# Query and key projections of a decoder layer branch round their low-half pass, with a common mantissa taken out of the scales

## Chip, cores and metric

One core of one Trainium2 chip runs the whole program. The metric is the device time of one execution in microseconds (us), from runs of the same program on the same inputs. TensorE (PE), VectorE (DVE), ScalarE (ACT), GpSimd (POOL) and SyncE (SP, which here only issues DMAs) each run their own list of instructions in order and wait for each other by semaphores.

## What is computed

A decoder layer with three parts, each followed by a residual sum and a layer norm: self-attention of 16 heads with a head dimension of 128 and 4-bit weights, a cross-attention with top-k, and a gated feed-forward part. Two sequences (b = 0, 1) of 512 tokens, model width 512. The change concerns the self-attention:

```python
def _mxfp4_matmul(x, codes, scales, block_size=BLOCK):
    w = codes * jnp.repeat(scales, block_size, axis=0)
    return x @ w
...
q = _mxfp4_matmul(x, wq_codes, wq_scales) + bq
k = _mxfp4_matmul(x, wk_codes, wk_scales) + bk
v = _mxfp4_matmul(x, wv_codes, wv_scales) + bv
...
scores = jnp.einsum('bqhd,bkhd->bhqk', q, k) / jnp.sqrt(jnp.float32(HEAD_DIM))
attn = jax.nn.softmax(scores, axis=-1)
```

A code is one of 0, 0.5, 1, 1.5, 2, 3, 4, 6 with a sign; a scale belongs to 32 rows of a column. In the inputs the scales of wv and wo are powers of two. Those of wq are powers of two times 2.869, those of wk powers of two times 2.863 (`factors` in the inputs' code), so each of these two tensors has one mantissa in all its 16 x 2048 scales.

## The kernel before

Every fp32 operand of a matmul is split in two halves of a reduced format: `hi`, a rounded copy, and `lo`, what the rounding left. A product is then three passes, lo by hi, hi by hi and hi by lo (`three`), and a 512-deep contraction of a 128 x 512 tile is 12 matmuls. Where the weight's `lo` is zero, one pass is nothing. For wv and wo the kernel tests this as it runs: `check_lo` notes the `lo` tile of each prepared piece, `run_checks` lets ACT sum its absolute values into a column of `mag`, `run_sums` adds the columns over partitions with a small matmul and puts the sum into `flag` by way of ACT, and `mm_if` loads the flag to a register of PE and branches round the matmuls with the weight's `lo` if it is zero. Before the change wq and wk pieces are not tested, and `proj_qk` always issues all 12.

A weight piece goes through `piece_a`: SP loads codes (`RAW`) and scales (`SCL`), POOL multiplies them, ACT writes `hi`, and POOL (DVE at the start and for wv) writes `lo`. The `lo` instruction is held back in `pend` until the next piece or until `flush`. Four `RAW`/`SCL` buffers rotate.

The attention is one loop over i = 4j + qt: j counts 32 pairs of head and sequence (`HB`), qt the four tiles of 128 queries. I call the four steps of one j a round. In this order the loop issues, for each step: the normalisation of the next tile (`recip`, `norm`, DVE), in the first two steps a projection for round j+1 (`proj_qk(j + 1, 0)` for q, then `(j + 1, 1)` for k), in the first step attention by values of round j-1 (`av`, 12 matmuls, which waits for the last transposed tile of that round), in the last two steps the output projection (`proj_o`, 4 matmuls with the branch taken round 2) and in 14 of the rounds a value projection (`proj_v`, 8 matmuls and 4 branched round), the transposes of tile i, the scores of tile i+2 (3 matmuls), then the evacuations by ACT (`hi`) and DVE (`lo`), the exponential of tile i+2 on ACT (`softexp`), and at the end the pieces to prepare. In the trace the instructions of a projection read R, those of `proj_v` read WV,R, those of `proj_o` WO,OT, those of `av` PT,V and those of the scores QK. DVE's row maximum of the scores is L405, its `norm` L422, its `lo` of the transposed tile L441, of a projection L340; ACT's exponential is L412. A projection's result goes to one of three PSUM banks in rotation (`fbank`).

Ahead of the loop stands a start written out by hand: load and prepare head 0, `proj_first`, two tiles of scores, the pieces of wv, then `prep_qk(1, 0)` and `prep_qk(1, 1)`, the four `proj_v(0, 0, tt)`.

Of the kernel before, what the change touches and what calls it, by code (L numbers as in the profile page):

```python
# [62 lines left out]
def decoder_layer(nc, xT, xn, wq, sq, wk, sk, wv, sv, wo, so, bqk, bv, bo,  # L63
                  xwq, xwo, ctxT, ctxn, scal, wg, wu, wd, out):
    with ExitStack() as top:
# [164 lines left out]
        def run_sums():  # L230
            while sums and sums[0][0] < now[0]:
                _, key = sums.pop(0)
                first, n, col, ts = FL[key]
                k, ps = fbank()
                o = ps[0:1, 0:n]
                t = pe.add(lambda e, o=o, first=first, n=n: e.matmul(o, ones[:, 0:1], mag[:, first:first + n],
                                                                  start=True, stop=True),
                           flat([ts, t_one, bank[5 + k]]), True)
                t = op(act, lambda e, o=o, col=col, n=n: e.activation(fsum[:, col, 0:n], o, ACT.Copy,
                                                                       accum_out=flag[:, col:col + 1]), t)  # L240
                bank[5 + k] = t
                T[("flag", *key)] = t

        def flag_of(key):
            c = FL[key][2]
            return flag[0:1, c:c + 1].bitcast(I32), T[("flag", *key)]

        def piece_a(key, hi, lo, src, ssrc, sview, free, em, el):
# [4 lines left out]
            ts = scl_s[k].load(SCL[:, k, 0:sview], ssrc, raw_free[k])  # L253
# [9 lines left out]
            def b():  # L263
# [3 lines left out]
                if key[0] != "qk":  # L267
                    check_lo(key, lo, tl)
# [927 lines left out]
```

How the kernel before makes its waits and increments, by code:

```python
    def emit(self, eng):  # L37
        reached = {}
        for waits, fn, inc in self.items:
            for sem, v in waits:
                if reached.get(id(sem), 0) < v:
                    reached[id(sem)] = v
                    eng.wait_ge(sem, v)
            if fn is None:
                continue
            ins = fn(eng)
            if inc:
                ins.then_inc(self.sem, 1)
# [33 lines left out]
            def load(self, dst, src, *waits):  # L82
                self.n += 1
                s = self.sem
                sp.add(lambda e: e.dma_start(dst, src).then_inc(s, 16), flat(waits), False)
                return (s, 16 * self.n)
```

## Time and profile before

| | |
|---|---|
| time, median of 3 runs | 1033.23 us (1032.26 to 1035.15) |
| profiled execution | 1032.74 us, of which the span from first to last instruction is 1030.8 us |
| mean granted TensorE clock | 0.988 |
| PE, weight loads, DVE, ACT, POOL busy | 94%, 77%, 63%, 51%, 39% |
| attention loop | from about 37 to 605 us of the span |

The profile page gives busy shares over the span and the chain of work that ended last. The trace behind it is read by stretches (windows), by groups of equal instructions, and as a timeline in which each row can end in the idle time before it and the instruction that ended it.

### The profile page before, as it was taken

The numbers are of one execution on the slowest core, as the hardware profiler recorded it, in microseconds if no ns is written. First come the engines' busy times: TensorE is split into PE (matmuls) and PEld (weight loads), VectorE is DVE, ScalarE is ACT, GpSimd is POOL, SyncE is SP. The second block draws the span as 40 slices with busy tenths as digits, with TensorE's granted clock in tenths as the row PEclk, the third lists the DMA queues.
The fourth block names the chain that finished last, engine by engine and source line by source line (L and its number), as shares of the span: only waits on it lengthen the run. The fifth ranks groups of instructions, "written<-read, shape, count | busy, mean of one in ns | idle before, by whom it ended". The sixth has DMA issues, their size and how long they took to land.

```text
span 1030.8 us, 13114 instructions
## 1 busy us (share of the span) xinstructions
PE 968.0 (94%) x4648; PEld 791.4 (77%) x4648; DVE 644.5 (63%) x1242; ACT 523.1 (51%) x1033; POOL 398.1 (39%) x313
## 2 busy tenths in 40 slices
PE   4899999999999999999999998979999899999996
PEld 3687777877787777787777777869888788788885
DVE  4557777676776586767687679986587613521113
ACT  3555564545654556546466546643474742543331
POOL 1233522223322134225434326753466662344440
PEclk9989999999999999999999999989999999999999
DMA  7321221011310022212212212232343342153331
GB/s 201 107 92 53 84 60 46 26 42 41 93 50 19 26 71 79 52 42 73 62 46 72 74 49 62 82 98 78 92 124 102 93 123 70 33 174 92 92 82 41
DMA packets 45665, 77.19 MB, mean 75 GB/s; under 512 B 5280, under 2 KB 10400, under 8 KB 45344
## 3 DMA queue, kind: packets, MB, share of 16 engines
q1 hardware_dynamic: 45600, 76.33, 25.5%
q8 instruction: 40, 0.66, 0.3%
q14 instruction: 25, 0.20, 0.1%
HBM read 74.21 MB, written 2.10 MB: 74 GB/s over the span
## 4 chain that ended last, share of the span: by engine, by line
PE 83%; DVE 12%; ACT 3%; issue 1%; POOL 0%; DMA 0%; SPq 0%; DVEq 0%; ACTq 0%; POOLq 0%
PE p L98 77%; PE p L431 5%; DVE PR L422 2%; DVE JK L405 2%; DVE QK L340 1%; DVE PT L441 1%; DVE st L490 1%; DVE m L628 1%; PE p L681 1%; DVE acc L392 0%; DVE WV L264 0%; DVE acc L504 0%; DMA SCL<-in_sk 0%; DVE OT L461 0%; PE p L538 0%
## 5 line engine op out<-in xcount | busy, mean ns | idle before, releaser
L98 PE MATMUL p<-R 128*128 128x512 f32 x768 | 190.4, 398 | 9.9 <-DVE R L480 9.9
L405 DVE TENSOR_SCALAR_CACHE_REDUCE JK<-p 128x512 bf16<-128x512 f32 x128 | 88.2, 689 | 146.9 <-PE p L98 146.8
L98 PEld LDWEIGHTS p<-R 128*128 128x128 f32 x768 | 147.3, 192 | 42.5 <-ACT R L479 9.8
L264 POOL TENSOR_TENSOR R<-RAW,R 128x512 fp32r<-128x512 f32 x38 | 51.3, 1351 | 247.0 <-ACT R L261 238.3
L412 ACT ACTIVATE PR<-p,nms 128x512 f32<-128x512 f32 x128 | 88.3, 690 | 105.2 <-DVE JK L405 105.2
L556 POOL TENSOR_TENSOR V<-RAW,V 128x512 fp32r<-128x512 f32 x64 | 82.3, 1306 | 143.5 <-ACT V L555 143.5
L98 PE MATMUL p<-QK 128*128 128x512 f32 x384 | 118.1, 416 | 6.0 <-ACT PR L412 4.4
L98 PE MATMUL p<-R,V 128*128 128x512 f32 x480 | 112.8, 390 | 0.7 <-ACT C L555 0.7
L98 PEld LDWEIGHTS p<-R,V 128*128 128x128 f32 x480 | 89.9, 188 | 19.8 <-issue 1.1
L260 POOL TENSOR_TENSOR RAW<-RAW,SCL 128x512 f32<-128x512 f32 x69 | 91.2, 1335 | 35.5 <-DMA SCL<-in_sv 13.9
L786 DVE TENSOR_TENSOR SX<-p,SX 128x512 f32<-128x512 f32 x32 | 22.1, 691 | 119.1 <-PE p L98 112.8
L422 DVE TENSOR_SCALAR PR<-PR,ri 128x512 f32<-128x512 f32 x128 | 92.7, 724 | 4.6
L98 PE MATMUL p<-WV,R 128*128 128x512 f32 x368 | 93.0, 400 | 1.9 <-ACT WV L261 1.8
L98 PE MATMUL p<-C 128*128 128x512 f32 x384 | 92.5, 390 | 0.0
L98 PE MATMUL p<-PT,V 128*128 128x512 f32 x384 | 92.5, 390 | 0.0
L556 POOL TENSOR_TENSOR C<-RAW,C 128x512 fp32r<-128x512 f32 x58 | 76.1, 1327 | 40.0 <-ACT C L555 40.0
L98 PE MATMUL p<-V 128*128 128x512 f32 (+1 forms) x432 | 90.9, 367 | 0.7 <-POOL V L556 0.7
L431 PE MATMUL p<-ident,PR 128*128 128x128 f32 x512 | 78.5, 276 | 13.5 <-DVE PR L422 13.4
L441 DVE TENSOR_TENSOR PT<-p,PT 128x512 fp32r<-128x512 f32 x128 | 87.1, 681 | 2.6 <-ACT PT L438 2.6
L431 PEld LDWEIGHTS p<-ident,PR 128*128 128x128 f32 x512 | 62.0, 141 | 33.9 <-DVE PR L422 20.3
L98 PEld LDWEIGHTS p<-WV,R 128*128 128x128 f32 x368 | 69.1, 191 | 21.6 <-DVE acc L392 4.3
L98 PEld LDWEIGHTS p<-V 128*128 128x128 f32 x432 | 74.5, 189 | 14.1 <-ACT V L555 1.1
(121 smaller groups left out, 1548.4 us busy)
## 6 DMA issues: line engine op xcount, KB each, us to landing
RAW<-in_wg SPq DMA_DIRECT2D x32, 256.0 KB, 2.9
RAW<-in_wu SPq DMA_DIRECT2D x32, 256.0 KB, 2.7
RAW<-in_ctxn SPq DMA_DIRECT2D x32, 256.0 KB, 2.8
RAW<-in_wd SPq DMA_DIRECT2D x32, 256.0 KB, 2.8
RAW<-in_wq SPq DMA_DIRECT2D x20, 256.0 KB, 2.7
RAW<-in_wk SPq DMA_DIRECT2D x20, 256.0 KB, 2.7
RAW<-in_wv SPq DMA_DIRECT2D x16, 256.0 KB, 2.8
SCL<-in_sv SPq DMA_DIRECT2D x16, 256.0 KB
```

The lines of the kernel that those rows point to most:

```text
L98: return e.matmul(outp, a, b, start=st, stop=sp_)
L260: tm = op(em, lambda e: e.tensor_tensor(rv, rv, sv_, ALU.mult), td, ts)
L264: tl = op(el, lambda e: e.tensor_tensor(lo, raw, hi, ALU.subtract), th, free)
L340: tl = op(dve, lambda e: e.scalar_tensor_tensor(out=lo, in0=ps, scalar=bias, in1=hi, op0=ALU.add, op1=ALU.subtract), th, free, T_BIAS)
L405: tm = op(dve, lambda e: e.tensor_scalar(JK[:, :], ps, -SC, None, ALU.mult, ALU.min, accum_out=m), T[("S", i)], T.get(("max", i - 1)), T.g ...
L412: T[("exp", i)] = op(act, lambda e: e.activation(PR[:, i % 3, :], ps, ACT.Exp, bias=m, scale=SC, accum_out=rs[:, i % 4:i % 4 + 1]), T[("ma ...
L422: T[("norm", i)] = op(dve, lambda e: e.tensor_scalar(p, p, ri[:, i % 4:i % 4 + 1], None, ALU.mult), T[("rec", i)])
L431: t = pe.add(lambda e, c=c: e.transpose(tp[:, c], PR[:, i % 3, c], ident[:, :]), flat([T[("norm", i)], free, t_id]) if kt == 0 else [], kt ...
L441: tl = op(dve, lambda e: e.tensor_tensor(lo, tv, hi, ALU.subtract), th, fr)
L490: ts = [op(dve, lambda e, r=r: e.bn_stats(st6[:, r, :], acc[:, r]), T[("acc", r)]) for r in rows]
L556: tl = op(pool, lambda e: e.tensor_tensor(lo, raw, hi, ALU.subtract), th, free)
L786: t = op(dve, lambda e: e.tensor_tensor(hf, u, hf, ALU.mult), T[("g", n, 1)], t)
```

## The change

A new function `factor`, run once near the start, finds out for wq and for wk whether all scales have the mantissa of the first one. It XORs the bits of all scales with the first, keeps the mantissa bits and takes the maximum, sums over partitions with a matmul, and makes a mask: all ones where they differ, sign and exponent alone where they agree. The masked scales are stored to two tensors in device memory, `rq` and `rk`, from which `prep_qk` takes its scales for every head but 0. The common mantissa goes, as a reciprocal, to a copy of the biases (`bqs`) and to a softmax scale held in memory (`ssc`). Head 0 keeps the old scales, bias and constant.

The pieces of wq and wk of all other heads are tested like those of wv and wo (two tests by ACT and one sum for each pair of pieces, q and k together), and `proj_qk` uses `mm_if` from j = 3 on but for head 0: 8 matmuls, and 4 more that are branched round. The pieces are prepared two steps earlier: in the last two steps of the round three ahead, in place of the first two steps of the round two ahead. `mag`, `fsum` and `flag` are laid out anew for 31 flags.

```diff
-        mag = sbt(top, "mag", [128, 48])
-        fsum = sbt(top, "fsum", [1, 12, 4])
-        flag = sbt(top, "flag", [1, 12])
+        mag = sbt(top, "mag", [128, 8, 4])
+        fsum = sbt(top, "fsum", [1, 4])
+        flag = sbt(top, "flag", [1, 32])
+        bqs = sbt(top, "bqs", [128, 32])
+        ssc = sbt(top, "ssc", [128, 2])
...
-            ts = scl_s[k].load(SCL[:, k, 0:sview], ssrc, raw_free[k])
+            ts = scl_s[k].load(SCL[:, k, 0:sview], ssrc, raw_free[k], ready)
...
-                if key[0] != "qk":
-                    check_lo(key, lo, tl)
+                if key[:2] != ("qk", 0):
+                    check_lo(key[:2], lo, tl)
...
-            src, ss = ((wq, sq), (wk, sk))[w]
+            src, ss = ((wq, rq if h else sq), (wk, rk if h else sk))[w]
...
-                    em or pool, el or pool)
+                    em or pool, el or pool, T[("scr", w)] if h else None)
...
-            pairs = []
+            pairs, extra = [], []
             for kt in range(4):
-                pairs += three(WQK[:, s, w, 0, kt], WQK[:, s, w, 1, kt], XT[:, b, 0, kt], XT[:, b, 1, kt])
-            xt = T[("xt", b)]
-            t = mm(ps, pairs, W[("qk", WJ[j], w)], bank[5 + k], at={3 * a: xt[2 * a:2 * a + 2] for a in range(4)})
+                wh, wl, xh, xl = WQK[:, s, w, 0, kt], WQK[:, s, w, 1, kt], XT[:, b, 0, kt], XT[:, b, 1, kt]
+                pairs += [(wh, xh), (wh, xl)]
+                extra.append((wl, xh))
+            if j < 2 or HB[j][0] == 0:
+                t = mm(ps, pairs + extra, W[("qk", WJ[j], w)], T[("xt", b)], bank[5 + k])
+            else:
+                f, t_f = flag_of(("qk", WJ[j]))
+                t = mm_if(ps, pairs, extra, "qk", f, None if w else t_f, W[("qk", WJ[j], w)], T[("xt", b)], bank[5 + k])
...
-            bias = bqk_t[:, w * 16 + h:w * 16 + h + 1]
+            bias = (bqs if h else bqk_t)[:, w * 16 + h:w * 16 + h + 1]
...
-            tm = op(dve, lambda e: e.tensor_scalar(JK[:, :], ps, -SC, None, ALU.mult, ALU.min, accum_out=m),
+            nsc = ssc[:, 1:2] if HB[j][0] else -SC
+            tm = op(dve, lambda e: e.tensor_scalar(JK[:, :], ps, nsc, None, ALU.mult, ALU.min, accum_out=m),
...
-                PR[:, i % 3, :], ps, ACT.Exp, bias=m, scale=SC, accum_out=rs[:, i % 4:i % 4 + 1]),
+                PR[:, i % 3, :], ps, ACT.Exp, bias=m, scale=sc, accum_out=rs[:, i % 4:i % 4 + 1]),
...
+        def factor_load():
+            t = None
+            for w, ss in enumerate((sq, sk)):
+                sc0_s.load(sr[:, w], ss.rearrange("a (b c) -> (a b) c", c=256))
+                t = sc0_s.load(ref[:, w:w + 1], ss[0:1, 0:1].to_broadcast((128, 1)))
+            return t
+
+        def factor(t_s):
+            td = []
+            for w in range(2):
+                a, x = sr[:, w].bitcast(I32), sx_[:, w].bitcast(I32)
+                t = op(dve, lambda e, a=a, x=x, w=w: e.tensor_tensor(
+                    x, a, refi[:, w:w + 1].to_broadcast((128, 256)), ALU.bitwise_xor), t_s)
+                t = op(dve, lambda e, x=x: e.tensor_tensor(x, x, k1.to_broadcast((128, 256)), ALU.bitwise_and), t, t_k1)
+                td.append(op(dve, lambda e, x=x, w=w: e.tensor_reduce(dif[:, w:w + 1], x, AX, ALU.max), t))
+            k, ps = fbank()
+            t = pe.add(lambda e: e.matmul(ps[:, 0:2], ones[:, 0:1].to_broadcast((128, 128)), dif, start=True, stop=True),
+                       flat([td, t_one, bank[5 + k]]), True)
+            tn = op(dve, lambda e: e.tensor_scalar(neq, ps[:, 0:2], 0.0, None, ALU.is_gt), t)
+            bank[5 + k] = tn
+            t = op(dve, lambda e: e.tensor_scalar(mski, neq, 8388607.0, -8388608.0, ALU.mult, ALU.add), tn)
+            for w in range(2):
+                a = sr[:, w].bitcast(I32)
+                tm = op(dve, lambda e, a=a, w=w: e.tensor_tensor(
+                    a, a, mski[:, w:w + 1].to_broadcast((128, 256)), ALU.bitwise_and), t)
+                T[("scr", w)] = scr_s[w].load((rq, rk)[w].rearrange("a (b c) -> (a b) c", c=256), sr[:, w], tm)
...
         prep_v(0, 3, dve, dve)
         flush()
+        t_s = factor_load()
         for kt in range(4):
             load_x(1, kt)
+        factor(t_s)
         recip(0)
         norm(0)
         prep_qk(1, 0)
...
-            if qt < 2 and j + 2 < NJ and WJ[j + 2] == j + 2:
-                todo.append(lambda: prep_qk(j + 2, qt))
+            if qt >= 2 and j + 3 < NJ and WJ[j + 3] == j + 3:
+                todo.append(lambda: prep_qk(j + 3, qt - 2))
```

What the change does to the order shows at two places. The first is PE between the first scores (reading QK) and the value projections of the start (WV,R); the program before, then the changed one. The new row is the matmul of `factor`.

```order
L98 MATMUL p<-R 128x512 x24
L98 MATMUL p<-QK 128x512 x6
L98 MATMUL p<-WV,R 128x512 x48
L98 MATMUL p<-R 128x512 x12
L431 MATMUL p<-ident,PR 128x128 x4
```

```order
L98 MATMUL p<-R 128x512 x24
L98 MATMUL p<-QK 128x512 x6
L853 MATMUL p<-BO,ones 128x2
L98 MATMUL p<-WV,R 128x512 x48
L98 MATMUL p<-R 128x512 x12
```

One small matmul stands ahead of all 48 matmuls of the value projections, and with it whatever it waits for on DVE.

On SP the same stretch follows; first before, then changed. SX and BO are used by `factor` for the scales and for small values, acc takes the second sequence.

```order
L85 DMA acc<-in_xT 128x512 x4
L85 DMA RAW<-in_wq 128x512
L85 DMA SCL<-in_sq 128x1x128
L85 DMA RAW<-in_wk 128x512
L85 DMA SCL<-in_sk 128x1x128
```

```order
L85 DMA SX<-in_sq 128x256
L85 DMA BO<-in_sq 128x1
L85 DMA SX<-in_sk 128x256
L85 DMA BO<-in_sk 128x1
L85 DMA acc<-in_xT 128x512 x4
L85 DMA rq<-SX 128x256
L85 DMA rk<-SX 128x256
L85 DMA RAW<-in_wq 128x512
L85 DMA SCL<-rq 128x1x128
L85 DMA RAW<-in_wk 128x512
L85 DMA SCL<-rk 128x1x128
```

Four loads are added ahead of the second sequence, and two stores ahead of the pieces of head 1, whose scales are now read back from what was stored.

The third is ACT where the pieces of head 6 for j = 12 are prepared (R<-RAW is the hi half of a piece, JA,mag a test of its lo half, PR the exponential). Before, in the first two steps of round 10:

```order
L337 ACTIVATE QK<-p,bqk_t 128x512
L458 ACTIVATE OT<-p,bv_t 128x512
L438 ACTIVATE PT<-p 128x4x128
L412 ACTIVATE PR,rs<-p,nms 128x512
L261 ACTIVATE R<-RAW 128x512
L337 ACTIVATE QK<-p,bqk_t 128x512
L438 ACTIVATE PT<-p 128x4x128
L412 ACTIVATE PR,rs<-p,nms 128x512
L261 ACTIVATE R<-RAW 128x512
```

In the changed program, from the end of the third step of round 9 to the second step of round 10:

```order
L265 ACTIVATE R<-RAW 128x512
L449 ACTIVATE PT<-p 128x4x128
L374 ACTIVATE V<-p 128x512
L423 ACTIVATE PR,rs<-p,nms,ssc 128x512
L265 ACTIVATE R<-RAW 128x512
L346 ACTIVATE QK<-p,bqs 128x512
L469 ACTIVATE OT<-p,bv_t 128x512
L449 ACTIVATE PT<-p 128x4x128
L423 ACTIVATE PR,rs<-p,nms,ssc 128x512
L228 ACTIVATE JA,mag<-R 128x512
L346 ACTIVATE QK<-p,bqs 128x512
L449 ACTIVATE PT<-p 128x4x128
```

The hi copies have moved two steps ahead, and where they stood there are now the two tests, each behind an exponential.

## Rows read from the trace of the kernel before

**Rows 1.** The page, busy time of TensorE: us, share of span, instructions

```profile
PE 968.0 (94%) x4648; PEld 791.4 (77%) x4648; DVE 644.5 (63%) x1242; ACT 523.1 (51%) x1033; POOL 398.1 (39%) x313
```

**Rows 2.** The page, the chain that ended last, shares by engine

```profile
PE 83%; DVE 12%; ACT 3%; issue 1%; POOL 0%; DMA 0%; SPq 0%; DVEq 0%; ACTq 0%; POOLq 0%
```

**Rows 3.** Windows, two rounds: stretch, length, busy us of each engine (instructions), clock, DMA

```profile
249.08:265.08 16.00, 15.05 (x74) 12.03 (x73) 11.60 (x27) 9.78 (x22) 3.73 (x4) 1.00 0.20 62
439.28:457.86 18.58, 18.58 (x89) 14.92 (x88) 13.41 (x28) 9.38 (x19) 5.27 (x4) 1.00 0.18 58
```

**Rows 4.** Timeline of a round with value projections: start, duration, engine, instructions

```profile
443.15 2.91 PE L98 MATMUL p<-R 128*128 128x512 f32 x12
...
445.89 0.60 PE L431 MATMUL p<-ident,PR 128*128 128x128 f32 x4
...
447.95 1.99 PE L98 MATMUL p<-WV,R 128*128 128x512 f32 x8
...
449.29 1.63 DVE L422 TENSOR_SCALAR PR<-PR,ri 128x512 f32<-128x512 f32 x1
449.34 1.30 POOL L264 TENSOR_TENSOR R<-RAW,R 128x512 fp32r<-128x512 f32 x1 [2.59 <-ACT R L261]
...
449.78 0.60 PE L431 MATMUL p<-ident,PR 128*128 128x128 f32 x4
...
452.47 1.70 PEld L98 LDWEIGHTS p<-WV,R 128*128 128x128 f32 x8 [0.35 <-DVE acc L392]
```

**Rows 5.** Timeline of a round without value projections, the same columns

```profile
253.14 0.69 DVE L405 TENSOR_SCALAR_CACHE_REDUCE JK<-p 128x512 bf16<-128x512 f32 x1 [3.59 <-PE p L98]
...
255.86 0.49 DVE L422 TENSOR_SCALAR PR<-PR,ri 128x512 f32<-128x512 f32 x1
...
257.03 0.69 DVE L405 TENSOR_SCALAR_CACHE_REDUCE JK<-p 128x512 bf16<-128x512 f32 x1 [0.68 <-PE p L98]
...
260.24 0.66 PE L431 MATMUL p<-ident,PR 128*128 128x128 f32 x4 [0.77 <-DVE PR L422]
...
262.36 2.88 PE L98 MATMUL p<-R 128*128 128x512 f32 x12
...
263.71 0.69 DVE L441 TENSOR_TENSOR PT<-p,PT 128x512 fp32r<-128x512 f32 x1
...
265.08 2.88 PE L98 MATMUL p<-PT,V 128*128 128x512 f32 x12
```

**Rows 6.** The sequencer instruction of the branches: ns minimum, median, maximum

```profile
L112 PEldq COMPARE_BRANCH  x92: 200/205/337, 63.5 to 618.6; - x92
```

**Rows 7.** Timeline of the start

```profile
23.57 0.54 SPq L85 DMA_DIRECT2D SCL<-in_sq  x1
...
24.30 1.47 DVE L264 TENSOR_TENSOR WV<-RAW,WV 128x512 fp32r<-128x512 f32 x2
...
25.09 11.42 PE L98 MATMUL p<-WV,R 128*128 128x512 f32 x42 [0.41 <-ACT WV L261]
...
27.47 2.52 POOL L260 TENSOR_TENSOR RAW<-RAW,SCL 128x512 f32<-128x512 f32 x2 [9.00 <-DMA SCL<-in_sq]
...
30.57 1.14 ACT L365 ACTIVATE V<-p 128x512 fp32r<-128x512 f32 x2
...
36.35 2.89 PE L98 MATMUL p<-R 128*128 128x512 f32 x12
```

**Rows 8.** DMA issues: KB each, median us to landing

```profile
out_x<-acc SPq DMA_DIRECT2D x8, 256.0 KB, 2.4
```

**Rows 9.** Groups by line: the tests of lo halves, busy us, mean ns

```profile
L224 ACT ACTIVATE JA<-WV 128x512 bf16<-128x512 f32 x16 | 9.9, 622 | 0.1
...
L224 ACT ACTIVATION_READ_ACCUMULATOR JA<-WV 128x1 f32 x16 | 3.0, 190 | 0.0
```

**Rows 10.** Windows of the start, granted clock in the third column from the right

```profile
26.00:28.00 2.00, 2.00 (x7) 1.58 (x6) 0.36 (x1) 0.00 (x0) 0.53 (x1) 0.54 0.83 259
28.00:30.00 2.00, 2.00 (x7) 1.55 (x6) 0.00 (x0) 0.63 (x1) 2.00 (x3) 0.61 0.82 198
```

More of the change, by code:

```diff
@@ L195, in decoder_layer @@
         bo_s = Slot("s_bo")
+        sc0_s = Slot("s_sc0")
+        scr_s = [Slot(f"s_scr{w}") for w in range(2)]
         raw_free = [None] * 4
@@ L232, in run_sums, with piece_a @@
                 _, key = sums.pop(0)
-                first, n, col, ts = FL[key]
+                n, col, ts = FL[key]
                 k, ps = fbank()
                 o = ps[0:1, 0:n]
-                t = pe.add(lambda e, o=o, first=first, n=n: e.matmul(o, ones[:, 0:1], mag[:, first:first + n],
-                                                                  start=True, stop=True),
+                t = pe.add(lambda e, o=o, col=col, n=n: e.matmul(o, ones[:, 0:1], mag[:, col % 8, 0:n],
+                                                                 start=True, stop=True),
                            flat([ts, t_one, bank[5 + k]]), True)
[L239 to L242, printed above, removed]
+                t = op(act, lambda e, o=o, col=col, n=n: e.activation(fsum[:, 0:n], o, ACT.Copy,
+                                                                       accum_out=flag[:, col:col + 1]),
+                       t, T.get(("flag", col - 1)))
+                bank[5 + k] = T[("flag", col)] = t
         def flag_of(key):
-            c = FL[key][2]
-            return flag[0:1, c:c + 1].bitcast(I32), T[("flag", *key)]
-        def piece_a(key, hi, lo, src, ssrc, sview, free, em, el):
+            c = FL[key][1]
+            return flag[0:1, c:c + 1].bitcast(I32), T[("flag", c)]
+        def piece_a(key, hi, lo, src, ssrc, sview, free, em, el, ready=None):
             n = npiece[0]
@@ L333, in evac_qk @@
             T[("proj", j, w)] = t
-            bias = bqk_t[:, w * 16 + h:w * 16 + h + 1]
+            bias = (bqs if h else bqk_t)[:, w * 16 + h:w * 16 + h + 1]
             hi, lo = QK[:, s, w, 0], QK[:, s, w, 1]
             free = T.get(("S", 4 * (j - 2) + 3))
-            th = op(act, lambda e: e.activation(hi, ps, ACT.Identity, bias=bias), t, free, T_BIAS)
+            th = op(act, lambda e: e.activation(hi, ps, ACT.Identity, bias=bias), t, free, T_BIAS, T.get(("bqs",)) if h else None)
             def lo_():
@@ L813, in ffn_end @@
                 T[("out",)] = out_s.load(out[r], acc[:, r], T[("acc", r)])
+        sr = SX0[:, 0:512].rearrange("p (w c) -> p w c", w=2)
+        sx_ = SX0[:, 512:1024].rearrange("p (w c) -> p w c", w=2)
+        tiny = BO[:, 0:64].rearrange("p (n c) -> p n c", c=2)
+        tinyi = BO[:, 0:64].bitcast(I32).rearrange("p (n c) -> p n c", c=2)
+        ref, dif, neq, cm, tmp, cc, rc = (tiny[:, i] for i in range(7))
+        refi, cmi, mski, k1 = tinyi[:, 0], tinyi[:, 3], tinyi[:, 7], tinyi[:, 8, 0:1]
@@ L848, in decoder_layer @@
         flush()
-        t_bo = bo_s.load(BO[:, :], bo.to_broadcast((128, 512)))
+        t_bo = bo_s.load(BO[:, :], bo.to_broadcast((128, 512)), T[("bqs",)], T[("ssc",)])
         def add_bo(r):
```

26 lines of the change are left out of this document (21 added, 5 removed).

## Prediction

> **What bounds the kernel now.** I read the page first: TensorE is busy for 968.0 of 1030.8 us [rows 1], and the chain that ended last runs on it for 83%, on DVE for 12% [rows 2]. The profiled execution took 1032.74 us, 1.9 us more than its span and within 0.05% of the median 1033.23, so I work from 1032.7. Within the attention loop I compared two rounds [rows 3]. A round with value projections takes 18.58 us with TensorE busy throughout. One without takes 16.00, of which 15.05 are busy, and DVE is busy for 11.60 there, so it is not far behind. The timelines say where each is ahead.
>
> In the round with value projections the projection (12 matmuls) starts at 443.15 and the next transposes at 445.89: 2.74 us, 0.228 a matmul [rows 4]. The durations of single rows are longer, since matmuls overlap; the starts count. In the other round DVE waits 3.59 us for the scores of the first step (253.14), behind 24 matmuls of projection and attention by values, and 0.68 us for those of the second (257.03). From there on it waits for nothing until the next round, and TensorE waits 0.77 us for DVE's norm (260.24) [rows 5]. So the first two steps are TensorE's, and the last two DVE's, if there is no value projection. The 14 rounds j = 1, 2, 6 to 9, 14 to 17, 22 to 25 have one, the other 18 not.
>
> **The branch.** All scales of a tensor share one mantissa, so with it gone a piece is code times power of two, its lo half zero and its flag zero. The program has 58 projections from j = 3 on: each leaves out 4 of 12 matmuls, 4 x 0.228 = 0.91 us. The ceiling is 58 x 0.91 = 52.9 us.
>
> The branch itself: 92 such instructions stand in the old program, 205 ns each on the sequencer [rows 6]. In the row at 447.95 one stands ahead of the eighth matmul, and the eight take 449.78 - 447.95 = 1.83 us, 0.229 each, as without a branch [rows 4]. I cost it at nothing. What hides it are matmuls already queued; bare, 58 x 0.205 = 12 us.
> The Trainium skill (Runtime: NRT & Kernel Launch, Instruction fetch mechanics) speaks against branches: a taken one whose target isn't in the window already fetched stalls until that page comes. These jumps are 4 matmuls long, and the trace of 92 of them disagrees with a stall at each.
>
> **What a round gives back.** Without a value projection, two savings of 0.91 us in each of the 16 rounds j = 3 to 5, 10 to 13, 18 to 21, 26 to 30. The first lies in DVE's wait of 3.59 us and counts, but attention by values follows the projection and waits for the last transposed tile. With 8 matmuls it could start 1.82 us after the projection, at 264.18 in place of 265.08; DVE's lo half of that tile ends at 263.71 + 0.69 = 264.40 [rows 5]. That leaves about 0.7. The second shortens DVE's wait of 0.68 us at most to nothing; where POOL has lengthened the norm ahead of it there is no such wait. I take 0.4 of 0 to 0.7. That is 1.1 a round, 17.6 us; in the last three rounds layer norm and cross-attention work already fills DVE, I take 1.5 off: 16.1.
>
> With value projections (13 rounds, from j = 2): TensorE is ahead throughout, but the sum of a pair's tests now takes a PSUM bank in the third step. Three banks rotate, so the output projection of the fourth step gets the bank of the third step's, which DVE must have added first. DVE is late there: TensorE already waited 0.35 us for that addition at 452.47, one group later in the order [rows 4]. With the sum inserted the wait comes 4 matmuls (0.9 us) earlier, less what DVE gains. Nine of the 13 rounds have such a sum (2, 6, 7, 14, 15, 22 to 25). I take 1.05 us for these and 1.7 for the other four: 16.3.
>
> The two tests of a pair cost ACT 2 x 0.75 us (0.62 and most of 0.19 [rows 9]), 19 pairs, 29 us in all. Each stands behind an exponential, where ACT next waits for TensorE; ACT is busy for 9.78 of 16.00 us [rows 3]. I cost them at nothing in the loop; if the cover goes, it is QK's or PT's hi half that is late, and 29 us are at stake. The added sums (0.3 us on ACT) stand in front of an exponential which at that time waits for DVE's maximum.
>
> The pieces are prepared two steps earlier. POOL's subtraction starts after the hi copy, just as DVE's norm does. At 449.29 the norm took 1.63 us against POOL's 1.30 at 449.34, and 0.49 with POOL idle [rows 4, 5]. Before, both subtractions of a pair met norms in DVE's tight stretch (second and third step); now the first one does and the second falls in the next round's first step, where DVE has its 3.59 us. I count 0, and up to 19 x 1.1 x 0.5 = 10 us of gain for the range.
> The Trainium skill (SBUF — State Buffer, SBUF: two separate sides) has the pair of ports that DVE and GpSimd share as an exclusive lock held for a whole instruction. By that rule each avoided meeting would give its 1.1 us in full, and the sum would be nearer 1000 than 1010; where a norm falls into a wait for TensorE it gives nothing.
>
> **The start.** This is what the change pays. DVE ends the wv pieces at 24.30 + 1.47 = 25.8 [rows 7] and then has six operations of 128 x 256 for the test of the mantissas. None is in the trace; the nearest is the 128 x 512 one, two of which took 1.47. Half of it (0.37) and all of it (0.73) are the ends, 2.2 to 4.4 us; I take 0.45, nearer the half, 2.7 us. The matmul of `factor` stands ahead of all value projections, so these start at 28.6; before, 42 of their 48 matmuls started at 25.09, the others earlier. Two small operations and the mask follow, and at about 29.8 SP issues the store of the masked scales. A store of 256 KB from SBUF lands after 2.4 us [rows 8]: 32.2. Only then SP can issue the load of head 1's scales. That load took from 23.57 to 27.47, 3.9 us [rows 7]: 36.1 to 36.2. From POOL's multiplication to ACT's first evacuation of a value projection it was 30.57 - 27.47 = 3.1 us, because ACT takes head 1's two hi copies first: 39.3. The fourth value projection needs the bank of the first, free after ACT (0.6) and DVE (0.7), at 40.7 with the waits; its 12 matmuls end at 43.5. Head 1's projection, at 36.35 before, starts at 43.7: 7.4 us.
> Then the two tests of head 1's pieces stand with the four of wv ahead of work that TensorE waited for: 1.5 us. Between 26 and 30 us, just after the wait that ended at 25.09, the granted clock was 0.54 and 0.61 [rows 7, 10], that is 1.2 GHz for most of it; the longer pauses move this stretch or add one, 0 to 2 us, I take 1. Start in all: 9.9, between 4.8 (the store and load quicker, no wait for the bank: 28.6 + 48 x 0.228 = 39.6, 3.3 late, and 1.5) and 14 (all slower). The constants that now come from memory (`ssc`, `bqs`) I cost at nothing; norm and exponential already have such operands.
>
> **Sum.** 1032.7 - 16.1 - 16.3 + 9.9 = 1010.2. The likeliest case spans 1001 to 1020.
>
> **Rivals.**
> *Nearly all counts:* DVE gains with TensorE, since shorter norms make up for what it lacks. Gross 42 to 53, net of the start 5 to 10: 985 to 1000. For it: no idle TensorE in rounds with value projections [rows 3]. Against: DVE has no waits in the last two steps [rows 5].
> *Little counts:* ACT's tests or full PSUM banks take the second projection's saving in every round and the start is long. 29 x 0.6 = 17 less 12: 1028; up to 1020 for milder forms. For it: 0.35 us waited for a bank already [rows 4].
> *The branches cost:* each of the 58 delays TensorE. The point from which this decides is (16.1 + 16.3 - 9.9)/58 = 0.39 us each. At a whole transfer of 2.4 us [rows 8] for fetched instructions it would be 139 us: 1149. Against: the row at 447.95, no delay. This is how the rule of the Trainium skill named above would come out.
> *ACT is blocked:* in rounds 24, 26 and 28 two pieces are prepared in each of two steps, and a hi copy waits in order for POOL, ahead of the next exponentials. The same in rounds 5 and 6, if POOL is behind: 18 prepared pairs x 2 us = 36 less the 22.5 gained: 1046. It decides from 1.25 us a pair. Against: POOL is busy for a quarter of a round [rows 3].
> *The flags aren't zero:* 12 matmuls as before, and the start's 9.9: 1043. Against: the inputs' code.
>
> **How the numbers follow.** Forecast 0.58; nearly all 0.15; little 0.13; branches cost 0.04; ACT blocked 0.07; flags 0.03. A measurement of this kernel tells about 0.3% (3 us) from no change. Faster: 0.58 + 0.15 + 0.11 = 0.84; same: 0.04, from the edges of "little" and "ACT blocked"; slower: 0.12. The range leaves out about 0.1 on either side: 993 to 1027.
>
> **What would show it.** The projections' rows: x8 with starts 1.8 us apart from the next transposes, 58 of them, and 232 matmuls fewer. PE's matmul of L853 near 28.6 us, head 1's projection near 43.7. Rounds without value projections near 14.9 us, those with at 16.9 to 17.5. COMPARE_BRANCH x150. The forecast is wrong if head 1's projection starts before 40 or after 48 us, if the rounds shorten by less than 0.7 or by the full 1.8 us, or if ACT shows waits for POOL in the loop.

## The result and the profile after

The changed kernel takes 1009.3 us (median of 4 runs, 1008.57 to 1010.6) against 1033.29: ratio 0.9767, 95% interval 0.975 to 0.9785. The forecast was 1010. Its profiled execution took 1009.04 us with a span of 1007.4, 23.4 less than before.

The page of the changed kernel, busy times and the chain that ended last [rows 1, 2]:

```profile
PE 925.1 (92%) x4456; PEld 751.7 (75%) x4456; DVE 643.9 (64%) x1262; ACT 555.0 (55%) x1147; POOL 395.0 (39%) x314
...
PE 73%; DVE 20%; ACT 3%; issue 1%; DMA 1%; POOL 1%; SPq 0%; DVEq 0%; ACTq 0%; POOLq 0%
```

TensorE is busy for 42.9 us less, the span fell by 23.4, and the chain's share on DVE went from 12% to 20%. What was left out and what came in, by groups of lines and by the branches' row [rows 6]:

```profile
L98 PE MATMUL p<-R 128*128 128x512 f32 x536 | 136.5, 399 | 10.5 <-DVE R L491 10.5
...
L228 ACT ACTIVATE JA<-R 128x512 bf16<-128x512 f32 x38 | 23.5, 620 | 0.4
...
L415 DVE TENSOR_SCALAR_CACHE_REDUCE JK<-p,ssc 128x512 bf16<-128x512 f32 x120 | 89.8, 748 | 109.5 <-PE p L98 109.3
...
L423 ACT ACTIVATE PR<-p,nms,ssc 128x512 f32<-128x512 f32 x120 | 93.4, 779 | 83.2 <-DVE JK L415 82.9
...
L433 DVE TENSOR_SCALAR PR<-PR,ri 128x512 f32<-128x512 f32 x128 | 81.7, 638 | 4.6
```

```profile
L112 PEldq COMPARE_BRANCH  x150: 200/205/341, 72.3 to 593.1; - x150
```

All 232 matmuls are gone (768 to 536) and the branches are 150. The row maximum (L415) and the exponential (L423), now with their scale from memory, have means of 748 and 779 ns where they had 689 and 690. The norm (L433) has 638 where it had 724.

I then cut the span at two points that both kernels have: the first attention by values, at the start of round j = 1, and the 31st, that of round j = 31, the last. The windows of the kernel before, then of the changed one (stretch, length, busy us of PE, PEld, DVE, ACT, POOL, granted clock, DMA share, GB/s):

```profile
0.00:57.75 57.75, 39.32 (x144) 30.36 (x145) 27.80 (x59) 26.34 (x55) 15.56 (x20) 0.91 0.59 171
57.75:582.46 524.71, 505.60 (x2427) 405.37 (x2426) 374.23 (x803) 291.84 (x635) 170.43 (x129) 1.00 0.18 53
582.46:1030.80 448.34, 423.04 (x2079) 355.70 (x2077) 242.50 (x380) 204.97 (x344) 212.14 (x166) 0.98 0.31 88
```

```profile
0.00:66.62 66.62, 38.89 (x148) 30.15 (x149) 32.74 (x79) 27.81 (x61) 14.13 (x20) 0.90 0.53 149
66.62:556.89 490.27, 460.34 (x2231) 363.54 (x2230) 368.76 (x803) 322.12 (x742) 169.31 (x130) 1.00 0.19 58
556.89:1007.40 450.51, 425.89 (x2079) 358.00 (x2077) 242.42 (x380) 205.06 (x344) 211.60 (x166) 0.98 0.30 88
```

The start is 8.9 us longer, the rounds between 34.4 shorter, the rest 2.2 longer. From the starts of attention by values I took the length of each round. The query projection of the next round stands ahead of attention by values, so a length holds the key projection for j + 1 and the query projection for j + 2: that of j = 1 has one of the 58 shortened projections, that of j = 30 one, those between have two.

| rounds | before | after | less |
|---|---|---|---|
| j = 1 | 16.7 | 15.8 | 0.9 |
| 9 with value projections and a sum of q and k (2, 6, 7, 14, 15, 22 to 25) | 168.9 | 162.8 | 6.1 |
| 4 with value projections, no such sum (8, 9, 16, 17) | 76.0 | 69.0 | 7.0 |
| 4 behind those with value projections (3, 10, 18, 26) | 66.2 | 55.8 | 10.4 |
| 9 other (4, 5, 11 to 13, 19 to 21, 27) | 142.6 | 134.5 | 8.1 |
| 3 last (28 to 30) | 54.3 | 52.4 | 1.9 |

The round j = 24 of the changed kernel, with value projections and a sum (timeline: start, duration, engine, instructions, idle before):

```profile
450.23 0.19 PE L240 MATMUL p<-mag,ones 128*1 128x2 f32 x2
...
451.01 0.69 DVE L401 TENSOR_TENSOR acc<-p,acc 128x512 f32<-128x512 f32 x1
...
451.75 1.19 PE L98 MATMUL p<-WO,OT 128*128 128x512 f32 x4 [0.75 <-DVE acc L401]
```

The sum (450.23) takes a bank, and the output projection of the fourth step (451.75) waits 0.75 us for DVE's addition of the one before (451.01). That is the wait that stood one group later, at 452.47, and was 0.35 us [rows 4]. The round j = 11, without value projections:

```profile
233.41 2.01 PE L98 MATMUL p<-R 128*128 128x512 f32 x8
...
237.59 0.74 DVE L349 SCALAR_TENSOR_TENSOR QK<-p,bqs,QK 128x512 fp32r<-128x512 f32 x1
...
238.48 0.93 PE L98 MATMUL p<-QK 128*128 128x512 f32 x3 [0.55 <-DVE QK L349]
...
238.86 1.27 POOL L264 TENSOR_TENSOR RAW<-RAW,SCL 128x512 f32<-128x512 f32 x1 [2.14 <-DMA SCL<-in_so]
...
239.04 1.38 DVE L433 TENSOR_SCALAR PR<-PR,ri 128x512 f32<-128x512 f32 x1
...
240.47 0.66 PE L442 MATMUL p<-ident,PR 128*128 128x128 f32 x4 [0.94 <-DVE PR L433]
...
242.60 2.00 PE L98 MATMUL p<-R 128*128 128x512 f32 x8
```

The projection of 233.41 has 8 matmuls. The scores of the third step (238.48) are the first tile of the next round and need the key projection's lo half, which DVE ends at 237.59 + 0.74 = 238.33: TensorE waits 0.55 us. Then the norm at 239.04 meets POOL's multiplication of 238.86 and takes 1.38 us, and TensorE waits for it at 240.47.

One round is longer than before, j = 30: 23.16 us against 21.84. TensorE waits there for 2.27 us until 544.41 (for 1.74 at the same place before), and then runs at a granted clock of 0.57 from 545 to 549, where the kernel before has 1.00. The window of 10 us from 543:

```profile
543.00:553.00 10.00, 8.53 (x37) 7.04 (x38) 8.73 (x17) 6.33 (x13) 2.05 (x2) 0.83 0.00 0
```

The start [rows 7]:

```profile
26.31 0.42 DVE L848 TENSOR_TENSOR SX<-SX,BO 128x256 int32<-128x256 int32 x1
...
28.46 0.42 DVE L851 TENSOR_REDUCE BO<-SX 128x1 f32<-128x256 int32 x1
...
28.98 0.56 PE L853 MATMUL p<-BO,ones 128*128 128x2 f32 x2 [6.66 <-DVE BO L851]
...
30.43 0.33 SPq L85 DMA_DIRECT2D rq<-SX  x1
...
32.15 0.53 SPq L85 DMA_DIRECT2D SCL<-rq  x1
...
36.18 1.28 POOL L264 TENSOR_TENSOR RAW<-RAW,SCL 128x512 f32<-128x512 f32 x1 [17.31 <-DMA SCL<-rq]
...
40.60 1.55 ACT L374 ACTIVATE V<-p 128x512 fp32r<-128x512 f32 x3
...
42.05 3.00 PE L98 MATMUL p<-WV,R 128*128 128x512 f32 x12 [2.30 <-DVE V L377]
...
44.89 2.89 PE L98 MATMUL p<-R 128*128 128x512 f32 x12
```

The matmul of `factor` waits for DVE until 28.98, and the value projections start at 29.4. The store of the masked scales is issued at 30.43, head 1's scales at 32.15, and POOL starts on them at 36.18. The fourth value projection waits for its bank (42.05), and head 1's projection starts at 44.89, where it was 36.35. One profile doesn't fix the length of a start: in the changed kernel, e1, e2 and e5 below, which issue the same instructions up to there (but for a constant in e5), the first attention by values came at 66.6, 66.6, 65.5 and 70.9 us, and at 57.8 and 54.7 in the kernel before and e4.

### The profile page after: what moved, and what is told of

The parts are those of the page before. It is cut to its first block, busy times and chain, and to the rows that moved or that the text cites. A ratio compares the mean times of both kernels' runs of the same rounds, so it can differ in the third digit from the quotient of the medians.

```text
span 1007.4 us, 12974 instructions
## 1 busy us (share of the span) xinstructions
PE 925.1 (92%) x4456; PEld 751.7 (75%) x4456; DVE 643.9 (64%) x1262; ACT 555.0 (55%) x1147; POOL 395.0 (39%) x314
## 4 chain that ended last, share of the span: by engine, by line
PE 73%; DVE 20%; ACT 3%; issue 1%; DMA 1%; POOL 1%; SPq 0%; DVEq 0%; ACTq 0%; POOLq 0%
PE p L98 69%; DVE JK L415 4%; PE p L442 3%; DVE PT L452 3%; DVE QK L349 2%; DVE PR L433 2%; DVE acc L401 2%; DVE OT L472 1%; DVE WV L268 1%; DVE st L501 1%; PE p L692 1%; PE p L549 1%; DMA SCL<-rk 1%; ACT JA L228 0%; DVE acc L515 0%
## 5 line engine op out<-in xcount | busy, mean ns | idle before, releaser
L415 DVE TENSOR_SCALAR_CACHE_REDUCE JK<-p,ssc 128x512 bf16<-128x512 f32 x120 | 89.8, 748 | 109.5 <-PE p L98 109.3
L98 PE MATMUL p<-R 128*128 128x512 f32 x536 | 136.5, 399 | 10.5 <-DVE R L491 10.5
L423 ACT ACTIVATE PR<-p,nms,ssc 128x512 f32<-128x512 f32 x120 | 93.4, 779 | 83.2 <-DVE JK L415 82.9
L98 PEld LDWEIGHTS p<-R 128*128 128x128 f32 x536 | 102.8, 192 | 33.5 <-ACT R L490 10.5
L797 DVE TENSOR_TENSOR SX<-p,SX 128x512 f32<-128x512 f32 x32 | 22.1, 691 | 119.9 <-PE p L98 114.3
L98 PEld LDWEIGHTS p<-PT,V 128*128 128x128 f32 x384 | 70.5, 188 | 22.0 <-issue 3.8
L433 DVE TENSOR_SCALAR PR<-PR,ri 128x512 f32<-128x512 f32 x128 | 81.7, 638 | 4.6
```

The costliest lines, as they stand in the source:

```text
L98: return e.matmul(outp, a, b, start=st, stop=sp_)
L415: tm = op(dve, lambda e: e.tensor_scalar(JK[:, :], ps, nsc, None, ALU.mult, ALU.min, accum_out=m), T[("S", i)], T.get(("max", i - 1)), T.g ...
L423: T[("exp", i)] = op(act, lambda e: e.activation(PR[:, i % 3, :], ps, ACT.Exp, bias=m, scale=sc, accum_out=rs[:, i % 4:i % 4 + 1]), T[("ma ...
L433: T[("norm", i)] = op(dve, lambda e: e.tensor_scalar(p, p, ri[:, i % 4:i % 4 + 1], None, ALU.mult), T[("rec", i)])
L797: t = op(dve, lambda e: e.tensor_tensor(hf, u, hf, ALU.mult), T[("g", n, 1)], t)
```

## The experiments

All times below are medians. The kernel before ran beside each group, at 1034 to 1036 us, so I compare ratios; "at 1033.3" is the ratio times 1033.3. The changed kernel stands at 0.9767 in a session of its own, so up to 2.5 us of each difference to it comes from that scaling. Round lengths come from one profile of each run; the rounds without value projections add up to 242.7, 243.8, 242.6 and 243.0 us in the changed kernel, e2, e6 and e11, so differences of such sums hold to about 1 us.

**e1_twelve.** All that the change brings, but no matmul left out:

```diff
-            if j < 2 or HB[j][0] == 0:
+            if True:
                 t = mm(ps, pairs + extra, W[("qk", WJ[j], w)], T[("xt", b)], bank[5 + k])
```

> The changed kernel, but every projection issues all 12 matmuls; tests, sums, factor, constants in memory and the earlier preparation stay. Theory A (each matmul left out saves 0.228 us where TensorE ends last, and the earlier preparation of the pieces is itself worth about 6 us, because POOL's subtraction then meets DVE's norm less often in the tight steps): 1033.3 + 8.9 (start) - 6 + 2 = 1038, between 1035 and 1041. Theory B (the earlier preparation is worth nothing, all of the loop's gain is the branch): 1042 to 1045.

1047.58 us, ratio 1.0119 (1.0103 to 1.0135), 1045.6 at 1033.3. Above both expectations, and nearer to theory B's. The difference to the changed kernel is what the branches bring: 0.0352, 36.4 us, and 39.5 between the two marks of the profiles. Its rounds say what else there is. Rounds 7, 15 and 23, with value projections and a sum, take 19.50 us where they took 18.56 and the changed kernel 17.7; 8 and 16, without a sum, take 18.6 as before and 16.8 in the changed kernel. So where TensorE ends last each projection gives its full 0.91 us (1.82 a round), and a sum costs 1.0. The rounds without value projections are 3.9 us shorter than before in all, with the same matmuls. That is the earlier preparation less the constants from memory, so the reason that theory B gave fell (e4 takes the preparation alone). I had added 2 us for tests, sums and constants, and nine sums alone are 9.

**e2_eight.** Eight matmuls, no branch, no register load:

```diff
-            if j < 2 or HB[j][0] == 0:
+            if j > 1 and HB[j][0]:
+                t = mm(ps, pairs, W[("qk", WJ[j], w)], T[("xt", b)], bank[5 + k])
+            elif True:
                 t = mm(ps, pairs + extra, W[("qk", WJ[j], w)], T[("xt", b)], bank[5 + k])
```

> The changed kernel with 8 matmuls in the projections from j = 3 on, without branch and register load; tests and sums stay (their flags of q and k are not read). Leaves out the case of a non-zero low half. Theory A (a branch behind queued matmuls costs TensorE nothing): within 1.5 us of 1009.3. Rival (each branch or register load delays TensorE): 0.1 us at each of 58 is 1003.5, 0.2 us 997.7.

1007.95 us, ratio 0.9743 (0.9729 to 0.9756), 1006.7 at 1033.3. By the ratio that is 2.5 us less than the changed kernel, a little more than the 1.5 of theory A and far from the 5.8 of the rival. The intervals of the two kernels overlap by a little, and between the same two marks the rounds took 491.5 us in the profile against 490.3 with branches. A branch costs TensorE nothing that shows in the loop.

**e3_sumbank.** The sums go to the bank of attention by values:

```diff
-                k, ps = fbank()
+                four = now[0] % 4 > 0
+                k, ps = (-1, P[4][:, :]) if four else fbank()
+                free4 = T.get(("ot", now[0] // 4 - 1)) if four else None
...
-                           flat([ts, t_one, bank[5 + k]]), True)
+                           flat([ts, t_one, bank[5 + k], free4]), True)
...
-            t = mm(ps, pairs, T[("v", G, b)], [T[("Tev", 4 * j + q)] for q in range(4)], T.get(("ot", j - 1)))
+            t = mm(ps, pairs, T[("v", G, b)], [T[("Tev", 4 * j + q)] for q in range(4)], T.get(("ot", j - 1)), bank[4])
```

> The changed kernel with the sums of the tests in PSUM bank 4 (that of attention by values, idle then) in place of one of the three rotating banks. Theory A (in the nine rounds with value projections and a sum, the output projection of the fourth step waits about 0.9 us for its bank, L98 <- DVE acc L401): those rounds fall from 17.7 or 18.1 to 16.8 to 17.2 us and the time to 1001 to 1003. Rival (those rounds lack DVE time or ACT's tests hold them): 1008 to 1010.

997.7 us, ratio 0.963 (0.9609 to 0.9652), 995.1 at 1033.3: 14 us less, more than expected. The same step of a round with value projections and a sum in its timeline:

```profile
443.30 0.75 DVE L417 TENSOR_SCALAR_CACHE_REDUCE JK<-p,ssc 128x512 bf16<-128x512 f32 x1 [1.08 <-PE p L98]
...
443.72 1.19 PE L98 MATMUL p<-WO,OT 128*128 128x512 f32 x4
...
444.71 1.69 PEld L98 LDWEIGHTS p<-WV,R 128*128 128x128 f32 x8 [0.24 <-DVE acc L403]
```

The output projection (443.72) no longer waits, and 0.24 us remain ahead of the value projection. Rounds 7, 15, 23 fell from 17.7 to 16.8 us, 6, 14, 22 from 18.1 to 17.2. Rounds 9, 17 and 25, in which the sum of a wo piece stood in the rotation, fell too (9 and 17 from 17.70 to 16.81, 25 from 18.81 to 17.47); in the kernel before they took 19.46 where round 8 took 18.5. The rounds with value projections are 10.5 us shorter in all. Round 29 is 1.6 us longer in this profile (16.93 against 15.32), with a granted clock of 0.57 from 520 to 524 us, so the other executions may well be faster than the profiled one; the rest of the 14 is not accounted for by rounds.

**e4_shift.** The kernel before, the pieces prepared two steps earlier:

```diff
-            if qt < 2 and j + 2 < NJ and WJ[j + 2] == j + 2:
-                todo.append(lambda: prep_qk(j + 2, qt))
+            if qt >= 2 and j + 3 < NJ and WJ[j + 3] == j + 3:
+                todo.append(lambda: prep_qk(j + 3, qt - 2))
```

> The kernel before with the one edit that the wq and wk pieces are prepared two steps earlier. Theory A: rounds 3, 10, 18 and 26 lose about 1.3 us each, in which a norm of 1.60 us (227.15, 366.49, 505.87) met POOL's subtraction, 1027 to 1029 in all. Theory B (rounds 3, 10, 18 and 26 gain 2.4 to 2.7 us from the projections alone): 1033.

1025.84 us, ratio 0.9912 (0.9897 to 0.9926): 9.1 us less, where theory A had 4 to 6. Rounds 10, 18 and 26 went from 16.52 to 15.39, round 3 only from 16.62 to 16.29, round 29 from 17.13 to 15.99, all rounds without value projections by 5.0 in sum, those with by nothing. In round 10 the norms of the second and third step took 0.96 and 1.59 us before, against POOL's subtractions. The second of them, and TensorE's wait for it, in the kernel before:

```profile
227.15 1.59 DVE L422 TENSOR_SCALAR PR<-PR,ri 128x512 f32<-128x512 f32 x1
227.19 1.27 POOL L264 TENSOR_TENSOR R<-RAW,R 128x512 fp32r<-128x512 f32 x1 [2.59 <-ACT R L261]
...
228.80 0.66 PE L431 MATMUL p<-ident,PR 128*128 128x128 f32 x4 [1.28 <-DVE PR L422]
```

In e4 both have POOL idle:

```profile
220.69 0.49 DVE L422 TENSOR_SCALAR PR<-PR,ri 128x512 f32<-128x512 f32 x1
...
223.92 0.49 DVE L422 TENSOR_SCALAR PR<-PR,ri 128x512 f32<-128x512 f32 x1
...
224.46 0.66 PE L431 MATMUL p<-ident,PR 128*128 128x128 f32 x4 [0.17 <-DVE PR L422]
```

TensorE's wait fell by 1.11 us, and the round by 1.13. Three more us of the profile lie in the start (first attention by values at 54.7 in place of 57.8), whose order the edit leaves alone but where the clock fell at other times (below); one profile each doesn't tell whether that holds for the other executions.

**e5_imm.** The softmax scale as a constant in the instructions:

```diff
-            nsc = ssc[:, 1:2] if HB[j][0] else -SC
+            nsc = -SC * 1.4345 * 1.4315 if HB[j][0] else -SC
...
-            sc = ssc[:, 0:1] if HB[i // 4][0] else SC
+            sc = SC * 1.4345 * 1.4315 if HB[i // 4][0] else SC
```

> The changed kernel with the softmax scale as a constant in the instructions (1.4345 x 1.4315 x SC, right for these inputs alone) in place of one read from memory. Row maximum and exponential then fall back from 0.748 and 0.779 us to 0.69 each. Theory A (DVE ends last in four steps of the 16 rounds without value projections, so 0.06 us counts there 64 times, and in the last steps of the others at times): 4 to 6 us less, 1003.5 to 1005.5. Rival (it lies in waits): 1009.

1002.94 us, ratio 0.9699 (0.9678 to 0.972): 7.0 us less. Both instructions are back at 689 ns:

```profile
L415 DVE TENSOR_SCALAR_CACHE_REDUCE JK<-p 128x512 bf16<-128x512 f32 x128 | 88.2, 689 | 121.5 <-PE p L98 121.1
...
L423 ACT ACTIVATE PR<-p,nms 128x512 f32<-128x512 f32 x128 | 88.2, 689 | 87.4 <-DVE JK L415 87.0
```

The rounds without value projections are 4.2 us shorter in sum, those with 0.6. Of the 4.2, 1.25 are in j = 30, where TensorE waits about as long as in the changed kernel (2.21 us) but the granted clock stays at 1.00 behind it; without that round the constants account for 3.6 us. The profiled execution was the slowest of the five, with a start 4.2 us later than the changed kernel's, so the profiles don't show where the rest of the 7.0 lies. By time, the constants that I had costed at nothing cost a little more than theory A said.

**e6_head1, e11_early.** Head 1 treated as head 0, so that its scales make no trip through memory; e6 also puts the matmul of `factor` and what follows behind the second value projection of the start, e11 leaves it ahead of them. What follows includes the two stores, which SP issues in order: in e11 they stay ahead of the loads of head 1's pieces, in e6 they come behind them. The core of the edit:

```diff
-            src, ss = ((wq, rq if h else sq), (wk, rk if h else sk))[w]
+            src, ss = ((wq, rq if h > 1 else sq), (wk, rk if h > 1 else sk))[w]
...
-            if j < 2 or HB[j][0] == 0:
+            if HB[j][0] < 2:
...
             proj_v(0, 0, tt)
             evacs()
+            if tt == 1:
+                factor_b(td_f, t_s)
```

> The changed kernel with head 1 treated as head 0 (old scales, bias and constant, no test, all 12 matmuls in j = 1 and 3), and the matmul of factor and what follows it placed behind the second value projection of the start. Theory A (the start's 8.9 us are the wait of TensorE at that matmul, the round trip of the masked scales through memory and two tests): 8.5 us less, 1.8 more for j = 3: 1002 to 1004. Rival (the start's delay is made up anyway by later waits): 1008 to 1010.

> As e6_head1 (head 1 treated as head 0), but with the matmul of factor left ahead of the value projections. Theory A: TensorE waits for it until 28.9 us, the value projections end near 40 and nothing else is late, so 3 to 4 us more than e6_head1's 1002.3: 1005 to 1006.5. Rival (the whole delay of the start was the round trip through memory): 1002 to 1003.

e6 1002.3 us, ratio 0.9699 (0.9672 to 0.9725); e11 1005.94, ratio 0.9721 (0.9699 to 0.9743). First attention by values at 59.2 and 62.5 us, 66.6 in the changed kernel, 57.8 before: of the 8.9 us, 4.1 went with the trip through memory and the two tests, 3.4 with the later matmul and stores. The 3.4 have two possible causes that no run separates: TensorE's wait at the matmul, and the stores ahead of head 1's loads on SP. In e11 the first of these scales is issued at 31.13 and POOL starts on it at 34.98; in e6 at 22.53 and 26.13. Round 2 takes 19.56, where the changed kernel took 18.80, as head 1's key projection is whole again. By time the two runs are 2.3 us apart, within their intervals, and starts of the same instructions lay up to 5 us apart above, so the shares of 4.1 and 3.4 are those of single executions. e11 against the changed kernel is clear by time: 4.8 us by the ratios, whose intervals don't meet. From e11:

```profile
28.34 0.56 PE L853 MATMUL p<-BO,ones 128*128 128x2 f32 x2 [6.66 <-DVE BO L851]
...
34.98 2.54 POOL L264 TENSOR_TENSOR RAW<-RAW,SCL 128x512 f32<-128x512 f32 x2 [15.72 <-DMA SCL<-in_sq]
...
42.35 2.88 PE L98 MATMUL p<-R 128*128 128x512 f32 x12
```

**e7_notest, e10_oldprep.** No tests and sums of wq and wk, 8 matmuls without a branch; e10 in addition prepares at the old place. Both have the edit of e2 and this one:

```diff
-                if key[:2] != ("qk", 0):
+                if key[0] != "qk":
```

> The changed kernel with 8 matmuls and no branch in the projections from j = 3 on, and also without the tests and sums of wq and wk. Leaves out the case of a non-zero low half. Theory A (the tests cost ACT time that is covered; what they cost is the bank of the sums, about 8 us, and 1.5 us at the start): 999 to 1001. Rival (ACT's tests delay evacuations in each round): below 996. Second rival (tests and sums are free): 1008 to 1009.

> The kernel without tests and branches (8 matmuls, e7_notest) with the wq and wk pieces prepared at the old place, the first two steps of the round two ahead. Theory A (POOL's subtractions meet norms where DVE has no slack, and with shorter projections the first two steps have less of it too): 8 to 12 us more than e7_notest's 998.4, 1006 to 1010. Rival (with fewer matmuls the meetings lie in other waits): 998 to 1001.

e7 998.42 us, ratio 0.9661 (0.9635 to 0.9687): 11.0 us under the changed kernel, 8.5 under e2, from which it differs by tests and sums alone; by the rounds 8.7, of which 8.3 in those with value projections. Its rounds with a sum of q and k fell to 16.8 and 17.2, to those of e3_sumbank, and the rounds without value projections are as long as with tests (243.4 and 242.7 us in sum). So the 38 tests cost ACT nothing that is seen; the bank does. e10 1002.99 us, ratio 0.9689 (0.9672 to 0.9705), 2.9 us more than e7 with intervals that touch, 3.7 by the rounds without value projections (10, 18, 26: 14.52 in place of 13.85). The earlier preparation is worth less here than in the old kernel, where I had expected more; the time lies between the two expectations for e10, near the rival's.

**e8_both, e9_floor.** e3 and e6 together; e9 with the constant of e5 too.

> Head 1 as head 0 with the matmul of factor later, and the sums in bank 4. Theory A: the two gains add, 993 to 997. Rival: they overlap or one of them is nothing, 1001 or more.

> Head 1 as head 0, sums in bank 4, and the softmax scale as a constant in the instructions (right for these inputs alone): the three gains of the runs before together. If they add: 993.4 - 7 = 986, between 984 and 989. If the constant's gain lay in rounds that the other two edits already shortened: 990 or more.

e8 993.39 us, ratio 0.9602 (0.958 to 0.9623), 992.2 at 1033.3: 17 us faster than the changed kernel, with all of its cases kept, and less than the 14 and 7 us of e3 and e6 added. Theory A's range, 993 to 997, held. e9 987.52, ratio 0.9543 (0.9522 to 0.9563): 6 us more, so the constants' 7.0 add to it within the intervals; it is right for these inputs' mantissas alone.

## Why the prediction was right

The sum was 32.4 us of gain less 9.9; the profile has 23.4, the medians 24.0. By its own steps:

**The branch.** 0.91 us a projection and nothing for the branch itself: both held (e1, e2). The rival that branches cost has no stall to show at 58 more of them. That doesn't contradict the Trainium skill (Runtime: NRT & Kernel Launch, Instruction fetch mechanics): it has a stall for a taken branch only where the target isn't in the window already fetched. How many of these jumps, each over 4 matmuls, left that window no run here shows; the rival took all 58.

**Rounds with value projections**, predicted 16.3, measured 13.1. The mechanism, the sum in the bank rotation, is shown by e3, with e7 beside it. Its size was off: I took 1.7 - 1.05 = 0.65 us for a sum, e1's rounds give 1.0. The wait comes four matmuls earlier, and I had let DVE gain time that shortens it; it gained none that shows. The four rounds without a sum gave the 1.7 each that I took. From e1 to the changed kernel, the branch alone, these rounds lose 22.1 us of the 23.7 that 26 projections could give.

**Rounds without them**, predicted 16.1, measured 20.4 from their lengths. The branch alone, from e1 to the changed kernel, gives 16.5 there, so this term held, but in part by luck: not 1.1 in each round, as I had it, but 6.9 in the four behind the value projections (1.7 each), 8.2 in the nine others (0.9 each) and 1.4 in the last three. Attention by values, which I had bound to the last transposed tile, waited for it only five times in the loop, 1.7 us in all, so the first saving was worth 0.9 and not 0.7; much of the second went into waits for DVE. I had left out that the third step's scores need the key projection's lo half from DVE; the row at 238.48 shows it, and no run separates its price. The step that was off is the earlier preparation, which I counted as 0 and kept 10 us for in the range. e4 shows 5.0 in these rounds of the old kernel, e10 and e7 3.7 in the new one. Against it stands a loss from the constants that I had as nothing: about 3 in these rounds by e5, and no more than about 1 in e1 with its 12 matmuls, where 3.9 of e4's 5.0 are left. The 16.5 and the 3.9 together are the 20.4. By the lock rule of the Trainium skill (SBUF — State Buffer, SBUF: two separate sides) each avoided meeting gives its 1.1 us; round 10 of e4 gives 1.13 for two meetings, one of which fell into a wait. The trace agrees with a lock (last section), and the caution of the forecast, that a meeting in a wait gives nothing, held too.

**The start**, predicted 9.9, measured 8.9, and 8.0 one round on. Step by step, with the forecast in brackets: DVE's six operations took 0.42 us each (0.45), the value projections started at 29.4 (28.6), the store let the next load go 1.7 us after its issue (2.4), the scales took 4.0 (3.9), ACT reached the evacuations 4.4 us after POOL began (3.1, as POOL here waits between the two pieces), head 1's projection started 8.5 late (7.4). The 1.5 us for the tests were to come on top; from head 1's projection to the first attention by values it took only 0.3 us longer than before (21.7 against 21.4). All of this is one pair of executions, and the spread of the starts is as large as its errors.

**The rest** was 2.2 us longer, which I hadn't counted. It is the same in every kernel here but for two constants, and its length from the 31st attention by values on was 448.3 us before, 450.5 in the changed kernel and between 447.8 and 450.7 in the other eleven profiles. So this is the spread of single executions as far as the runs show.

**Signs.** 150 branches, the matmul of `factor` and head 1's projection came where they were announced. Two signs of a wrong forecast showed in part: nine rounds shortened by 0.68 us on average (less than 0.7) and j = 30 not at all, while 3, 10, 18 and 26 shortened by 2.4 to 2.7 (more than 1.8, the preparation on top of the branch). ACT waited for POOL with a hi copy three times in the loop, 3.5 us in all, so the rival of a blocked ACT is at most a trace.

The errors nearly cancel, which is luck. As additions to the forecast time: +3.2 in the rounds with value projections, -4.3 in those without, -1.0 in the start, -0.9 in round j = 1, +2.2 in the rest, in all -0.8; the sum said 22.5 less and the profile says 23.4. The -0.9 is no gain that I had missed but the place of the cut: round j = 1 holds a projection that I had counted in a later one.

What stays open: e3 gained 14 us by its ratio, 11.6 by the medians as they stand and 10.4 by the spans of the two profiles; e4 9.1, 7.3 by its spans and 5.0 by its rounds. The clock, at the start and behind waits in the last rounds, is one candidate, not shown. Open is also how the start's loss divides between TensorE's wait at the matmul and SP's order.

## What to carry to other kernels

When work is taken from the bounding engine, price what the test for it borrows, not only its instructions: here 38 tests on ACT were free, while one small sum in a rotation of three PSUM banks cost 1.0 us a time, and a bank that is idle then gave that back. A result that is needed early should not go through device memory on the way if the few consumers near the start can do without it, and a store that waits for such a result holds up the loads behind it in the same queue. Look at what moves along with the edit: preparing POOL's pieces two steps earlier was worth 3.7 to 5.0 of the loop's 34.4 us. Check a sum that came out by its terms: here an unpriced gain and an underpriced loss hid each other.

## What the runs showed of the hardware

- A scale read from memory in place of a constant in the instruction lengthened the row maximum of 128 x 512 on DVE from 689 to 748 ns and the exponential on ACT from 690 to 779; e5 took both back to 689.
- A norm (128 x 512, SBUF to SBUF, on DVE) takes 0.49 us with POOL idle. Of those lengthened in the changed kernel's loop, 31 ended 0.28 or 0.29 us after the end of the POOL instruction that they had met, whenever they had begun: at 239.04 + 1.38 = 240.42 against 238.86 + 1.27 = 240.13. Where the norm began first it kept its 0.49, and POOL's instruction took 1.44 in place of 1.29 (POOL's at 230.22, the norm at 230.02). A row maximum, which reads PSUM, kept its 0.68 us at 228.66 in the kernel before, with POOL busy throughout.
- Behind a wait of TensorE of about the same length the clock can fall or stay: in round j = 30 it was 0.57 from 545 to 549 us in the changed kernel, after 2.27 us, and 1.00 from 545 to 549 in e5, after 2.21 us.
- The clock at the start falls at different times in executions of the same instructions. Windows of the kernel before, then of e4_shift, whose start has the same order (granted clock in the third column from the right):

```profile
24.00:28.00 4.00, 3.59 (x11) 2.61 (x12) 2.23 (x5) 0.63 (x1) 0.53 (x1) 0.77 0.79 205
28.00:32.00 4.00, 4.00 (x16) 3.23 (x15) 0.82 (x2) 2.31 (x4) 4.00 (x4) 0.80 0.92 245
48.00:52.00 4.00, 1.02 (x7) 0.95 (x7) 2.74 (x7) 2.58 (x8) 0.00 (x0) 0.76 0.15 27
52.00:56.00 4.00, 4.00 (x12) 3.13 (x11) 2.92 (x8) 2.84 (x7) 1.57 (x2) 0.50 0.89 317
```

```profile
24.00:28.00 4.00, 4.00 (x20) 3.27 (x19) 0.78 (x3) 0.63 (x1) 2.25 (x2) 1.00 0.77 201
28.00:32.00 4.00, 4.00 (x19) 3.31 (x18) 1.97 (x3) 2.21 (x4) 2.80 (x3) 1.00 1.04 253
48.00:52.00 4.00, 3.91 (x12) 3.24 (x13) 3.19 (x9) 2.53 (x7) 1.28 (x1) 0.50 0.80 284
52.00:56.00 4.00, 4.00 (x15) 3.25 (x14) 0.65 (x2) 1.24 (x3) 3.37 (x3) 0.77 0.88 285
```

The first attention by values came 3.1 us apart, and 5.4 us apart in four kernels with the changed start (65.5 to 70.9). One execution doesn't measure a start to better than that.
